# Key side of a two-block attention kernel: every second slot in the order gathering, transposes, keys

## The chip, the cores and the metric

The kernel runs on one core of one Trainium2 chip. The metric is the device time of one execution in microseconds (us), as the median of several runs; lower is better.

## The reference, cut to what matters

The whole program is four residual blocks on `x` (32 batches x 64 x 512): attention, feed-forward, a second attention, and a projection with a small expert mixture. The change touches only work that depends on the context and the weights, and not on `x`: the key side of the second attention block, which this kernel computes first.

```python
def _L1_xattn_ref(q, k, v, Wq, Wk, Wv, Wo, bo, g):     # q from x, k = v = ctx: (32, 64, 512)
    kh = jnp.einsum('bcn,oc->bon', k, Wk).reshape(b, HEADS, DIM_HEAD, -1)
    vh = jnp.einsum('bcn,oc->bon', v, Wv).reshape(b, HEADS, DIM_HEAD, -1)
    kh = jax.nn.softmax(kh, axis=-1)
    context = jnp.einsum('bhdn,bhen->bhde', kh, vh)
    ...
    out = jnp.einsum('bhde,bhdn->bhen', context, qh)
    ...
    out = jnp.einsum('bcn,oc->bon', out, Wo) + bo[None, :, None]
```

The key side yields for each batch a matrix `k.M` that holds `context`, the value weights and `Wo` in one product.

## The kernel before

`program` (L1703) runs the stages one after the other: `key_side` (L214), `attention0`, `feed_forward`, `query_side`, `projection`, `experts`. Each stage is a block in which every engine has a queue of its own, written out by hand; semaphores (`wait_ge`, `then_inc`) are all that orders one engine against another. A stage begins when all engines have left the one before it.

`key_side` works on 16 tiles `t`, each of two batches (128 rows of the context), and each tile in four chunks `c`. The steps of a tile are these, with the line of the instruction:

- `context` (TensorE, L607): four transposes of the context into the bank `psM`; ScalarE copies them to `cT` (`transposed`, L551).
- `keys(t, c)` (TensorE, L617): six matmuls, 64x128 weights against 512 columns, into `psK[c % 2]`, a pair of banks for each of two buffers. Then `keys_max` (VectorE, L411) takes the row maxima, and `exponentials` (ScalarE, L558, two activations with accumulation) writes `ek`. The same buffer of `psK` is written again two chunks later, once the exponentials have read it.
- `turn(t, j, b)` (TensorE, L628): four transposes of `ek` into `psT[b]`, for b = 0 and 1. The copies to `eT` are `turned` on VectorE (L416) for b = 1, and for b = 0 an activation on ScalarE (L586); only at the last chunk, j = 3, is b = 0 VectorE's too.
- `gather(t, j)` (TensorE, L640): two matmuls, 128x64 weights against 512 columns, which add chunk j into the bank `psG`. There is one `psG`: after j = 3 ScalarE copies it to `gT` (L592), and `gather(t, 0)` waits for the copy of the tile before (`gT_ok`, L635).
- `matrix(t)` (TensorE, L649): eight small products of `gT` into `psM`, then one VectorE instruction (L426) into `k.M`. It waits for `gT_ok` and, as `psM` is shared with `context`, for `transposed` of tile t + 2 (`cT_ok`, L646).

The main loop goes over laps `t` (0 to 16) and slots `c` (0 to 3). Slot c of lap t holds the keys of the chunk that lies five chunks ahead, `keys(t + 1 + (c + 1) // 4, (c + 1) % 4)`: chunks 1, 2 and 3 of tile t + 1 in slots 0, 1, 2, and chunk 0 of tile t + 2 in slot 3. TensorE's queue in a lap is: slot 0 keys, transposes, `gather(t - 1, 3)`; slot 1 keys, transposes, `gather(t, 0)`, `context(t + 1)`; slot 2 keys, transposes, `gather(t, 1)`, `matrix(t - 1)`; slot 3 keys, transposes, `gather(t, 2)`.

VectorE's queue follows it: in each slot `keys_max` and then `turned`, with single tasks between (`low`, the low halves of the context, L406; weight magnitudes, L433, in the first laps; statistics of `x`, L440, from lap 6 on). ScalarE's queue in a slot is: copy of `psT[0]` (slots 0 to 2), then the exponentials; in slot 0 behind them the copy to `gT`, in slot 1 behind them the copy to `cT`; in laps 0 to 5 weight magnitudes (L567) behind the exponentials of slots 2 and 3 (in lap 5 only slot 2). GpSimd makes the high halves of the context (L364) and from lap 7 on casts the feed-forward weights (L371 to L376), which SyncE's queue then transposes by DMA.

Of the kernel before, what the change touches and what calls it, by code (L numbers as in the profile page):

```python
# [30 lines left out]
NC = L // P  # L31
BATCHES = 32
TILES = BATCHES * D // P
# [18 lines left out]
def chunk(ap, c, n=P):  # L52
    return ap[:, c * n:(c + 1) * n]
# [7 lines left out]
def wait(eng, sem, value):  # L61

    if not isinstance(value, int) or value > 0:
        eng.wait_ge(sem, value)
# [149 lines left out]
def key_side(nc, a, k):  # L214

    with ExitStack() as ctx:
# [41 lines left out]
        def sums_at(t):  # L258
            return range(3 * t, min(3 * t + 3, UNITS))
# [142 lines left out]
        def _(dve):  # L402
            def low(t):
                dve.wait_ge(hi_ok, t + 1)
                wait(dve, k_ps, NC * (t - 1))
                dve.tensor_tensor(cs_lo[t % 2][:, :], cf[t % 2][:, :], cs_hi[t % 2][:, :], ALU.subtract).then_inc(lo_ok, 1)  # L406

            def keys_max(t, c):
                dve.wait_ge(k_ps, NC * t + c + 1)
                wait(dve, ek_ok, 2 * NC * (t - 1) + 2 * c + 2)  # L410
                dve.tensor_reduce(mk[:, c, :], psK[c % 2][:, :, :], X, ALU.max, negate=True).then_inc(mk_ok, 1)  # L411

            def turned(t, j, b):
                dve.wait_ge(t_ps, 2 * NC * t + 2 * j + b + 1)
                wait(dve, g_ps, NC * (t - 1) + j + 1)
                dve.tensor_copy(eT[b][:, j, :], psT[b][:, :]).then_inc(eT_dve, 1)  # L416

            def sums(t):
                dve.wait_ge(ek_ok, 2 * NC * t + 2 * NC)
                wait(dve, M_ok, t - 1)  # L420
                dve.reciprocal(rl[t % 2][:, :, :], le[t % 2][:, :, :]).then_inc(rl_ok, 1)

            def matrix(t):
                dve.wait_ge(rl_ok, t + 1)
                dve.wait_ge(m_ps, t + 1)
                dve.tensor_tensor(k.M[:, 2 * t:2 * t + 2, :, :], psM[:, :].rearrange("p (c b d) -> p b c d", b=2, d=D),  # L426
                                  rl[t % 2][:, :, :].unsqueeze(3).broadcast_to([P, 2, NC, D]), ALU.mult).then_inc(M_ok, 1)

            def magnitudes(u):
                dve.wait_ge(k.unit_in[u % RING], loads_of(u))  # L430
                n, blocks, src = unit_of(a, u)
                room = unit_room(k, u)
                dve.tensor_reduce(k.wabs[0:room.shape[0], n, u % PAIRS:u % PAIRS + 1], room, X, ALU.add,  # L433
                                  apply_absolute_value=True).then_inc(wa_dve, 1)
# [16 lines left out]
            def biases(n):  # L451

                if n == 0:
                    dve.wait_ge(k.b_in, 16 * 2)
                    dve.tensor_copy(part[:, :, :], brow[:, :, :]).then_inc(row_ok, 1)
                    dve.wait_ge(row_ok, 1)
                    dve.tensor_tensor(rest[:, :, :], brow[:, :, :], part[:, :, :], ALU.subtract).then_inc(row_ok, 1)
                    spread(0, part)
                elif n == 1:
                    dve.wait_ge(row_ok, 4)  # L460
                    dve.tensor_copy(part[:, :, :], rest[:, :, :]).then_inc(row_ok, 1)
                    dve.wait_ge(row_ok, 5)
                    dve.tensor_tensor(rest[:, :, :], rest[:, :, :], part[:, :, :], ALU.subtract).then_inc(row_ok, 1)
                    spread(32, part)
                else:
                    dve.wait_ge(row_ok, 6)
                    spread(64, rest)

            def scales():
                dve.wait_ge(sum_ps, 1)  # L470
                dve.tensor_scalar(k.wmean[:, :], psM[:, 0:3], 1.0 / (FF * L), None, ALU.mult).then_inc(inv_ok, 1)
                dve.wait_ge(inv_ok, 1)
                dve.tensor_scalar(den[:, :], k.wmean[:, :], EPS, None, ALU.add).then_inc(inv_ok, 1)
                dve.wait_ge(inv_ok, 2)
                dve.reciprocal(k.winv[:, :], den[:, :]).then_inc(inv_ok, 1)
# [38 lines left out]
            keys_max(1, 0)  # L514
            for t in range(TILES + 1):
                for c in range(NC):
                    if t + 1 + (c + 1) // NC < TILES:
                        keys_max(t + 1 + (c + 1) // NC, (c + 1) % NC)
                    if t < TILES:
                        if c == NC - 1:  # L520
                            turned(t, c, 0)
                        turned(t, c, 1)
                    if c == 0 and t < TILES:
                        sums(t)
                    if c == 0 and 1 <= t < 4:
                        biases(t - 1)
                    if c == 1 and t + 2 < TILES:
                        low(t + 2)
                    if c == 2 and t > 0:
                        matrix(t - 1)  # L530
                    if c == 3:
                        for u in sums_at(t):
                            if u % 3 == 2:
                                magnitudes(u)
                    if c == 0 and t == CAST - 1:
                        dve.wait_ge(wa_act, UNITS - UNITS // 3)
                        dve.wait_ge(wa_dve, UNITS // 3)
                        dve.tensor_reduce(asum[:, :], k.wabs[:, :, :], X, ALU.add).then_inc(sum_ok, 1)
                    if c == 0 and t == CAST:
                        scales()  # L540
                    if c in (0, 3) and STATS <= t < STATS + TILES // 2:
                        stats(2 * (t - STATS) + c // 3)
                    if c == 1 and t == TILES - 1:
                        vec_x(dve)
# [56 lines left out]
        def _(pe):  # L601
            def context(t):

                pe.wait_ge(lo_ok, t + 1)
                wait(pe, M_ok, t - 2)
                for c in range(NC):
                    mm = pe.transpose(chunk(psM, c), chunk(cf[t % 2], c), k.ident[:, :])  # L607
                mm.then_inc(c_ps, 1)

            def keys(t, c):  # L610

                pe.wait_ge(lo_ok, t + 1)
                wait(pe, ek_ok, 2 * NC * t + 2 * c - 2)
                products = ((k.wk_hi, cs_hi[t % 2]), (k.wk_hi, cs_lo[t % 2]), (k.wk_lo, cs_hi[t % 2]))
                for n, (w, x) in enumerate(products):
                    for b in range(2):
                        mm = pe.matmul(psK[c % 2][:, b, :], w[HALF[b], c * P:(c + 1) * P], x[HALF[b], :],  # L617
                                       start=n == 0, stop=n == 2)
                mm.then_inc(k_ps, 1)
# [11 lines left out]
            def gather(t, j):  # L631

                if j == 0:
                    pe.wait_ge(cT_ok, t + 1)
                    wait(pe, gT_ok, t)  # L635
                if j < NC - 1:
                    pe.wait_ge(eT_act, (NC - 1) * t + j + 1)
                pe.wait_ge(eT_dve, 5 * t + j + 1 + j // (NC - 1))
                for b in range(2):
                    mm = pe.matmul(psG[HALF[b], :], cT[t % 2][:, j, b * D:(b + 1) * D], eT[b][:, j, :], start=j == 0,  # L640
                                   stop=j == NC - 1)
                mm.then_inc(g_ps, 1)
# [56 lines left out]
            pe.wait_ge(w_ok, VO_OK)  # L699
            for t in range(TILES + 1):  # L700
                for c in range(NC):
                    if t + 1 + (c + 1) // NC < TILES:
                        keys(t + 1 + (c + 1) // NC, (c + 1) % NC)
                    if t < TILES:
                        turn(t, c, 0)
                        turn(t, c, 1)
                    if c > 0 and t < TILES:
                        gather(t, c - 1)
                    if c == 0 and t > 0:
                        gather(t - 1, NC - 1)  # L710
                    if c == 1 and t + 1 < TILES:
                        if t == CAST:
                            pe.wait_ge(inv_ok, 1)
                        context(t + 1)
                    if c == 2 and t > 0:
                        matrix(t - 1)
                    if c == 3 and t == CAST - 1:
                        pe.wait_ge(sum_ok, 1)
                        pe.wait_ge(M_ok, t)
                        pe.matmul(psM[:, 0:3], k.ones32[:, :], asum[:, :], start=True, stop=True).then_inc(sum_ps, 1)  # L720
# [1073 lines left out]
```

## Time and profile before

| | us |
|---|---|
| median of 3 runs | 799.75 (798.72 to 800.43) |
| the profiled execution, its device time | 799.84 |
| its span in the trace | 797.8 |
| main loop of the key side, within the span | 22.2 to 223 |

Engines are PE (TensorE matmuls), PEld (its weight loads), DVE (VectorE), ACT (ScalarE), POOL (GpSimd). A view of the stretches of time gives for each engine its busy time and the number of its instructions, then TensorE's granted clock as a share of full speed. In a timeline a row is: start in us, time in us, engine, line, operation, tile written and tiles read, shape, number of instructions merged; a bracket behind it is idle time of that engine before it and what ended that. A row of x8 lasts from the first start to the last end. Ends overlap the next start, since matmuls are pipelined: what a step costs is read from start to start.

### The profile page before, as it was taken

What the parts mean: (1) busy time and instruction counts of PE and PEld (TensorE: products, weight loads), DVE (VectorE), ACT (ScalarE), POOL (GpSimd) and SP (SyncE); (2) the same over time, 40 slices, a digit from 0 to 9 for tenths busy, and PEclk for the clock granted to TensorE, in tenths of its full rate; (3) what the DMA queues carried; (4) which work ended last, traced back from release to release, by engine and by line L of the source; (5) the groups of instructions that cost most, each with busy time, mean ns of one, the idle gap of its engine ahead of it and who ended that gap; (6) DMA issues with size and microseconds to landing.
All of it is one profiled execution on the core that took longest, in us unless ns stands there. A gap on an engine that the chain in (4) does not pass through costs nothing. (4 is left out here: it accounts for less than half of the span.)

```text
span 797.8 us, 17690 instructions
## 1 busy us (share of the span) xinstructions
PE 691.3 (87%) x6633; PEld 358.0 (45%) x6633; DVE 622.4 (78%) x1031; ACT 482.2 (60%) x870; POOL 364.8 (46%) x271
## 2 busy tenths in 40 slices
PE   4999999999967875699999489999999999389944
PEld 2454455545545654244444144444444444145541
DVE  6888788888636676699998398999999999355456
ACT  3878876676436665476776167878788787422100
POOL 2000039999725563022112257767686767333100
PEclk9999999999999998799999779999999999779955
DMA  6235455656253320134332100000000000045305
GB/s 161 77 132 171 154 177 151 152 135 173 55 146 72 83 68 6 21 75 75 75 67 57 31 0 2 1 2 1 2 1 1 2 1 1 1 80 80 53 1 210
DMA packets 94183, 54.90 MB, mean 69 GB/s; under 512 B 78548, under 2 KB 78548, under 8 KB 94100
## 3 DMA queue, kind: packets, MB, share of 16 engines
q1 hardware_dynamic: 93348, 53.25, 26.7%
q8 instruction: 54, 0.88, 0.5%
q10 hardware_dynamic: 752, 0.52, 0.3%
q14 instruction: 29, 0.24, 0.1%
HBM read 32.20 MB, written 4.19 MB: 46 GB/s over the span
## 5 line engine op out<-in xcount | busy, mean ns | idle before, releaser
L1312 POOL TENSOR_TENSOR query_qn<-query_eq,query_rq 128x1024 f32<-128x1024 f32 x64 | 121.8, 1904 | 56.7 <-DVE query_rq L1246 54.9
L558 ACT ACTIVATE keys_ek<-keys_psK,keys_mk 128x512 f32<-128x512 f32 x128 | 86.9, 684 | 38.9 <-DVE keys_mk L411 37.0
L411 DVE TENSOR_REDUCE keys_mk<-keys_psK 128x2 f32<-128x1024 f32 x64 | 77.9, 1217 | 16.7 <-PE keys_psK L617 16.6
L1237 DVE TENSOR_REDUCE query_mq<-query_psQ 128x16 bf16<-128x1024 f32 x64 | 75.6, 1181 | 5.2 <-PE query_psQ L1380 5.0
L1243 DVE TENSOR_REDUCE query_lq<-query_eq 128x16 f32<-128x1024 f32 x64 | 77.2, 1207 | 2.6 <-ACT query_eq L1321 2.5
L1321 ACT ACTIVATE query_eq<-query_psQ 128x1024 f32<-128x1024 f32 x64 | 65.2, 1019 | 22.5 <-PE query_psQ L1393 22.5
L628 PE MATMUL keys_psT<-all_ident,keys_ek 128*128 128x128 f32 x512 | 70.8, 282 | 0.0
L1402 PE MATMUL query_psX<-all_ident,query_qn 128*128 128x128 f32 x512 | 70.7, 282 | 0.0
L1040 POOL TENSOR_SCALAR ff_hr<-ff_h,ff_qs 128x1376 f32<-128x1376 f32 x16 | 22.7, 1416 | 104.4 <-DVE ff_qs L1087 104.4
L640 PE MATMUL keys_psG<-keys_eT,keys_cT 128*64 128x512 f32 x256 | 69.0, 617 | 1.0 <-issue 0.9
L628 PEld LDWEIGHTS keys_psT<-all_ident,keys_ek 128*128 128x128 f32 x512 | 55.5, 142 | 28.2 <-issue 20.0
L1328 ACT ACTIVATE query_qT<-query_psX 128x1024 f32<-128x1024 f32 x64 | 65.4, 1022 | 1.2 <-PE query_psX L1402 1.2
L1412 PE MATMUL query_psF<-query_qT,all_M 128*64 128x512 f32 x256 | 61.8, 604 | 1.1 <-ACT query_qT L1328 1.1
L1402 PEld LDWEIGHTS query_psX<-all_ident,query_qn 128*128 128x128 f32 x512 | 55.5, 142 | 15.7 <-issue 14.3
L376 POOL TENSOR_SCALAR keys_st<-all_ring 128x1024 bf16<-128x1024 f32 (+2 forms) x16 | 60.7, 3796 | 1.3
L1161 PE MATMUL ff_psG<-all_wgT,ff_xT 128*128 128x512 bf16 (+1 forms) x192 | 46.8, 367 | 10.6 <-DMA ff_xT<-ff_xq 10.6
L416 DVE COPY keys_eT<-keys_psT 128x512 f32<-128x512 f32 x80 | 53.1, 680 | 2.9 <-PE keys_psT L628 2.9
L364 POOL TENSOR_SCALAR keys_cs_hi<-all_cf 128x512 f16<-128x512 f32 x16 | 9.9, 621 | 97.0 <-DMA all_cf<-in_ctx_dram 88.2
L1134 ACT ACTIVATE ff_r<-ff_psG,all_sg 128x512 f32<-128x512 f32 (+1 forms) x48 | 30.9, 643 | 36.3 <-PE ff_psG L1161 34.6
L1535 PE MATMUL proj_psH<-all_ring,proj_x_T 128*128 128x512 f16 x192 | 46.1, 392 | 0.0
L1166 PE MATMUL ff_psU<-all_wuT,ff_xT 128*128 128x512 bf16 (+1 forms) x192 | 46.1, 363 | 0.0
L1175 PE MATMUL ff_psD<-all_wdT,ff_hT 128*128 128x512 bf16 (+1 forms) x176 | 42.1, 389 | 4.1 <-DMA ff_hT<-ff_hq 4.1
(246 smaller groups left out, 1438.6 us busy)
## 6 DMA issues: line engine op xcount, KB each, us to landing
all_ring<-in_L_ffn_w_down_dram SPq DMA_DIRECT2D x8, 688.0 KB, 4.7
all_ring<-in_L_ffn_w_gate_dram SPq DMA_DIRECT2D x10, 512.0 KB, 4.9
all_ring<-in_L_ffn_w_up_dram SPq DMA_DIRECT2D x10, 512.0 KB, 3.9
all_x_res<-in_x_dram SPq DMA_DIRECT2D x4, 1024.0 KB, 6.1
att_ctx_n<-in_ctx_dram SPq DMA_DIRECT2D x16, 256.0 KB, 2.9
out_dram<-all_x_res SPq DMA_DIRECT2D x16, 256.0 KB, 2.2
all_cf<-in_ctx_dram SPq DMA_DIRECT2D x15, 256.0 KB, 2.6
att_w_nat<-in_L_ffn_W_dram SPq DMA_DIRECT2D x4, 256.0 KB, 4.5
```

The costliest lines, as they stand in the source:

```text
L376: pool.tensor_scalar(st[v % 2][:, 0:w], r, -ROUND, 0.0, ALU.add, ALU.add).then_inc(cast_ok, 1)
L411: dve.tensor_reduce(mk[:, c, :], psK[c % 2][:, :, :], X, ALU.max, negate=True).then_inc(mk_ok, 1)
L558: act.activation(ek[t % 2][b][:, c, :], psK[c % 2][:, b, :], ACT.Exp, bias=mk[:, c, b:b + 1], accum_out=le[t % 2][:, b, c:c + 1]).then_inc ...
L628: mm = pe.transpose(chunk(psT[b], c), chunk(ek[t % 2][b][:, c, :], j), k.ident[:, :])
L640: mm = pe.matmul(psG[HALF[b], :], cT[t % 2][:, j, b * D:(b + 1) * D], eT[b][:, j, :], start=j == 0, stop=j == NC - 1)
L1237: dve.tensor_reduce(mq[g % 2][:, :, 0:HEADS], psQ[g % 2][:, :, :].rearrange("p b (h d) -> p b h d", d=D), X, ALU.max, negate=True).then_in ...
L1243: dve.tensor_reduce(lq[:, :], eq[g % 3][:, :, :], X, ALU.add).then_inc(lq_ok, 1)
L1312: pool.tensor_tensor(qn[m % 2][:, :, :], eq[m % 3][:, :, :], rq[m % 2][:, :].unsqueeze(2).broadcast_to([P, 2 * HEADS, D]), ALU.mult).then_ ...
L1321: act.activation(eq[g % 3][:, :, :].rearrange("p h d -> p (h d)"), psQ[g % 2][:, :, :].rearrange("p b n -> p (b n)"), ACT.Exp).then_inc(eq ...
L1328: act.activation(qT[t % 2][:, :, c * P:(c + 1) * P], psX[:, :, :].rearrange("p b (j n) -> p (b j) n", n=P), ACT.Copy).then_inc(qT_ok, 1)
L1402: mm = pe.transpose(psX[:, b, j * P:(j + 1) * P], qn[g % 2][:, b * HEADS + 2 * j:b * HEADS + 2 * j + 2, :].rearrange("p h d -> p (h d)"), ...
L1412: mm = pe.matmul(psF[HALF[b], :], k.M[:, 2 * t + b, j, :], qT[t % 2][:, b * NC + j, :], start=j == 0, stop=j == NC - 1)
```

## The change

The slots with odd c get another order. On TensorE the gathering of the slot comes first, then its transposes, then (in slot 1) `context`, and the keys last. Slots 0 and 2 keep theirs. On VectorE `keys_max` moves behind `turned` in the same slots, 1 and 3. ScalarE's, GpSimd's and SyncE's queues are as before, and no instruction is added or removed.

A lap on TensorE then reads: keys, transposes, `gather(t - 1, 3)` | `gather(t, 0)`, transposes, `context(t + 1)`, keys | keys, transposes, `gather(t, 1)`, `matrix(t - 1)` | `gather(t, 2)`, transposes, keys.

```diff
@@ VectorE, lap t, slot c @@
-                    if t + 1 + (c + 1) // NC < TILES:
+                    if c % 2 == 0 and t + 1 + (c + 1) // NC < TILES:
                         keys_max(t + 1 + (c + 1) // NC, (c + 1) % NC)
                     if t < TILES:
                         if c == NC - 1:
                             turned(t, c, 0)
                         turned(t, c, 1)
+                    if c % 2 == 1 and t + 1 + (c + 1) // NC < TILES:
+                        keys_max(t + 1 + (c + 1) // NC, (c + 1) % NC)
@@ TensorE, lap t, slot c @@
-                    if t + 1 + (c + 1) // NC < TILES:
+                    if c % 2 == 1 and t < TILES:
+                        gather(t, c - 1)
+                    if c % 2 == 0 and t + 1 + (c + 1) // NC < TILES:
                         keys(t + 1 + (c + 1) // NC, (c + 1) % NC)
                     if t < TILES:
                         turn(t, c, 0)
                         turn(t, c, 1)
-                    if c > 0 and t < TILES:
-                        gather(t, c - 1)
-                    if c == 0 and t > 0:
-                        gather(t - 1, NC - 1)
                     if c == 1 and t + 1 < TILES:
                         if t == CAST:
                             pe.wait_ge(inv_ok, 1)
                         context(t + 1)
+                    if c % 2 == 1 and t + 1 + (c + 1) // NC < TILES:
+                        keys(t + 1 + (c + 1) // NC, (c + 1) % NC)
+                    if c == 2 and t < TILES:
+                        gather(t, c - 1)
+                    if c == 0 and t > 0:
+                        gather(t - 1, NC - 1)
                     if c == 2 and t > 0:
                         matrix(t - 1)
```

## Rows read from the trace of the kernel before

**Rows 1.** The page: span, TensorE's busy share, its granted clock in 40 slices
```profile
span 797.8 us, 17690 instructions
...
PE   4999999999967875699999489999999999389944
...
PEclk9999999999999998799999779999999999779955
```

**Rows 2.** Stretches of time: laps in the key side, and attention0 behind it
```profile
60.00:110.00 50.00, 49.25 (x359) 24.98 (x357) 39.87 (x56) 39.43 (x95) 2.48 (x4) 1.00 0.51 167
135.00:185.00 50.00, 50.00 (x368) 25.68 (x368) 42.46 (x65) 33.38 (x84) 48.65 (x31) 1.00 0.58 141
224.00:314.00 90.00, 66.81 (x2686) 49.89 (x2686) 57.95 (x109) 53.94 (x91) 49.06 (x52) 0.96 0.33 83
```

**Rows 3.** Timeline of TensorE: laps 3 and 4, slots 1 to 3 and on
```profile
61.94 1.09 PE L628 MATMUL keys_psT<-all_ident,keys_ek 128*128 128x128 f32 x8
63.22 1.08 PE L640 MATMUL keys_psG<-keys_eT,keys_cT 128*64 128x512 f32 x4 [0.19 <-issue]
64.23 0.66 PE L607 MATMUL keys_psM<-all_ident,all_cf 128*128 128x128 f32 x4
64.82 0.39 PE L617 MATMUL keys_psK<-keys_cs_hi,all_wk_hi 64*128 64x512 f16 x2
65.05 0.38 PE L617 MATMUL keys_psK<-keys_cs_lo,all_wk_hi 64*128 64x512 f16 x2
...
65.57 1.09 PE L628 MATMUL keys_psT<-all_ident,keys_ek 128*128 128x128 f32 x8
66.59 1.08 PE L640 MATMUL keys_psG<-keys_eT,keys_cT 128*64 128x512 f32 x4
67.50 1.04 PE L649 MATMUL keys_psM<-all_wv_wo,keys_gT 128*64 128x128 f32 x16
68.48 0.39 PE L617 MATMUL keys_psK<-keys_cs_hi,all_wk_hi 64*128 64x512 f16 x2
...
81.09 0.39 PE L617 MATMUL keys_psK<-keys_cs_hi,all_wk_hi 64*128 64x512 f16 x2
```

**Rows 4.** Timeline of VectorE, lap 3
```profile
65.68 1.22 DVE L411 TENSOR_REDUCE keys_mk<-keys_psK 128x2 f32<-128x1024 f32 x1 [0.85 <-PE keys_psK L617]
...
69.34 1.23 DVE L411 TENSOR_REDUCE keys_mk<-keys_psK 128x2 f32<-128x1024 f32 x1
70.48 1.28 DVE L416 COPY keys_eT<-keys_psT 128x512 f32<-128x512 f32 x2
```

**Rows 5.** Timeline of ScalarE, laps 3 and 4
```profile
62.53 0.59 ACT L592 ACTIVATE keys_gT<-keys_psG 128x512 f32<-128x512 f32 x1
63.01 0.60 ACT L586 ACTIVATE keys_eT<-keys_psT 128x512 f32<-128x512 f32 x1
...
66.94 0.69 ACT L558 ACTIVATE keys_ek<-keys_psK,keys_mk 128x512 f32<-128x512 f32 x1
...
68.28 1.05 ACT L567 ACTIVATE keys_st<-all_ring 128x1024 bf16<-128x1024 f32 x1
...
71.94 1.05 ACT L567 ACTIVATE keys_st<-all_ring 128x1024 bf16<-128x1024 f32 x1
...
72.99 0.59 ACT L586 ACTIVATE keys_eT<-keys_psT 128x512 f32<-128x512 f32 x1
73.52 0.69 ACT L558 ACTIVATE keys_ek<-keys_psK,keys_mk 128x512 f32<-128x512 f32 x1
```

**Rows 6.** Timeline of TensorE, lap 5, slot 1
```profile
87.41 1.09 PE L628 MATMUL keys_psT<-all_ident,keys_ek 128*128 128x128 f32 x8
89.06 1.08 PE L640 MATMUL keys_psG<-keys_eT,keys_cT 128*64 128x512 f32 x4 [0.56 <-issue]
```

## The prediction

> **What bounds the kernel now.** I read the page first for where TensorE is the bound, then the stretches of time, then the timelines of TensorE, VectorE and ScalarE over one lap. The page shows TensorE at nine tenths or more, at full clock, over most of the key side [rows 1]. By stretches it is stricter: TensorE is busy for 49.25 of 50 us in laps 3 to 6 and 50.00 of 50 later, at a granted clock of 1.00, while VectorE has about 40 and ScalarE 33 to 39 of 50 [rows 2]. So in the key side TensorE's own queue sets the pace, and what it has not got is room for a wait. From the keys of slot 3 in lap 3 (68.48) to those in lap 4 (81.09) a lap takes 12.61 us [rows 3].
>
> The timeline of TensorE gives the step from each group to the next: keys to transposes 0.75, transposes to gathering 1.02, gathering to `matrix` 0.91, `matrix` to keys 0.98, gathering to `context` 1.01, `context` to keys 0.59 [rows 3]. Two things can be read from these steps. First, the gathering costs 0.91 when `matrix` follows, whose weights have the same 128x64 shape, and 1.01 when `context` (128x128) follows: about 0.10 us is lost where the shape changes. Second, four transposes alone (`context`) cost 0.59 and eight cost 1.02, so four cost 0.43 and a lone group of them 0.16 more, at its two borders together. A pair of key matmuls takes 0.23 at the head of a group [rows 3]; three pairs without a border are about 0.66.
>
> The waits of today stand in the same rows. `gather(t, 0)` once started 0.26 us later than its 1.02 (61.94 to 63.22): ScalarE's copy `gT` had begun at 62.53, and the gathering began 0.69 after it [rows 3, 5]. In lap 5 the same step is 1.65, so 0.63 late [rows 6]. The same 0.26 occurs in lap 1. This wait on the one bank `psG` is thus already the latest thing before slot 1's gathering, even with a whole key group and the transposes (0.75 + 1.02) between `gather(t - 1, 3)` and `gather(t, 0)`. The change takes this cover away.
>
> **The change, part by part.**
>
> *Borders on TensorE.* Before, a lap has 13 changes of shape (four keys to transposes, four transposes to gathering, gathering to keys twice, gathering to `context`, `context` to keys, `matrix` to keys). After, it has 8: in slots 0 and 2 keys to transposes and transposes to gathering, in slots 1 and 3 gathering to transposes, then `context` or transposes to keys; the pairs keys-keys, gathering-gathering, transposes-`context`, gathering-`matrix` and `matrix`-gathering have equal shapes. Five borders at 0.10 to 0.16, taken as 0.13, are 0.66 us a lap; 15 laps give -9.9. Keys behind keys, gathering behind gathering and transposes behind gathering are orders that no row shows; from below they save nothing (0), from above 5 x 0.16 = 0.8 a lap. I take 0.66, since the one equal-shape neighbour that the rows have, gathering to `matrix`, has no border in spite of a wait at its head.
>
> The Trainium skill, "TensorEngine Tiling (Array Packing)", section Key Properties, says that changing the tiling mode drains TensorE. The trace agrees as far as the 0.91 against 1.01 goes. By this rule alone the change would be a gain: that is the rival of the other sign, below.
>
> *The wait on `psG`.* `gather(t - 1, 3)` now ends slot 0 and `gather(t, 0)` begins slot 1, with nothing between them. The second may not write `psG` before ScalarE has copied it, and on ScalarE that copy is queued behind the exponentials of `keys(t + 1, 1)`. The keys of slot 3 and slot 0 are now adjacent, so all that work comes in one burst. Counting from the start of slot 3's keys: 0.86 until VectorE begins the maxima (64.82 to 65.68), 1.26 until the exponentials begin (to 66.94), 1.34 for them (to 68.28), 0.53 for slot 0's copy of `psT[0]` (72.99 to 73.52), 1.34 for the exponentials of slot 0, 0.69 for the copy `gT` up to the gathering [rows 3 to 5]. The sum is 6.02; with some hundredths for the hand-overs 6.1. VectorE's way is as long where statistics or other small work lie between its maxima (0.86 + 1.14 + some 0.8 + 1.26 + 1.34 + 0.69 = 6.1, with 1.14 from 69.34 to 70.48) [rows 4]. TensorE needs from the same point 0.66 (keys) + 0.75 (keys) + 1.02 (transposes) + 0.91 (gathering) = 3.34. The wait is 2.75 us in laps 6 to 14. In laps 1 to 5 a weight magnitude stands behind slot 3's exponentials on ScalarE, 1.05 (71.94 to 72.99) [rows 5], and the wait is 3.8. Lap 15 has no keys in slot 0, and about 0.9 remains. Together 5 x 3.8 + 9 x 2.75 + 0.9 = 44.7. Queued behind the waiting gathering are slot 1's transposes, `context` and both key groups, and on these VectorE and ScalarE wait in turn: nothing catches the loss up, as the next burst starts from keys that come behind it.
>
> *The wait of `matrix`.* It needs `cT` of `context(t + 1)`, and ScalarE makes it behind the exponentials of slot 1's keys, which TensorE now does last. From the start of those keys: 0.86 + 1.26 + 1.34 + 0.69 = 4.15 [rows 3 to 5], against 0.66 + 0.75 + 1.02 + 0.91 = 3.34 on TensorE. The wait is 0.8 us, in 14 laps 11.3.
>
> *Ends.* In lap 0 `gather(0, 0)` comes straight behind its transposes and waits for their copy, about 0.9; later `gather(0, 2)`, directly ahead of which no `matrix` lies yet, about 1.4. In lap 15 most groups have no keys beside them and wait for copies of 0.6 to 0.7, about 2.2 in all. Together 4.5, bounds 2 and 7. The old waits, 0.26 + 0.26 + 0.63 = 1.15, are inside the new ones and are taken off.
>
> *What is hidden.* `keys_max` moved behind `turned` costs nothing on its own: it moves with its keys. Both VectorE (40 of 50) and ScalarE have time in a lap of 15.5 us [rows 2]. GpSimd's and SyncE's queues aren't touched; in laps 9 to 12 GpSimd is busy for 48.65 of 50 us [rows 2], which would hold back a faster lap, while a lap of 15.5 gives it room, and its casts end before TensorE does. The buffers `psK` come free in time: a key group waits for exponentials two groups back, and these are over before the wait on `psG` is.
>
> **The sum.** -9.9 + 44.7 + 11.3 + 4.5 - 1.2 = +49.4 us. As a cross-check, a lap follows from its chain: 6.1 (keys of slot 3 to `gather(t, 0)`), then 0.96 + 0.93 + 0.53 for gathering, transposes and `context` with their single borders, 4.15 (keys of slot 1 to `matrix`), then 0.86 + 0.96 + 1.02 to the keys of slot 3: 15.5 us against 12.6. The profiled execution took 799.84, its span 797.8, and the median is 799.75, so the same sum stands on either: 799.8 + 49.4 = 849.2, rounded to 849.5 for the hand-overs left out.
>
> **The rivals.**
>
> *The clock falls too.* TensorE is then idle for 3.6 of 15.5 us (23%), where it had been busy throughout. In attention0, where it is busy for 66.81 of 90 us, the granted clock was 0.96 [rows 2], that is, short times at its lower level of 1.2 GHz. At 0.96 over the 250 us of the new key side 20 us would be spent at half clock; some 40% of a lap's chain is TensorE work, each such us of it doing half: 20 x 0.4 x 0.5 = 4, so about 854; with longer falls, as the page shows elsewhere (0.5 to 0.7 of a slice) [rows 1], 860 or more. The Trainium skill, "TensorE: Matmul & The Clock Gate", section A second HAM failure mode: psum-queue depth-cycling, tells of small idle times between groups of matmuls that make the clock go up and down; no run here shows it in this stage.
>
> *A border belongs to every group, not to a change of shape.* Then the -9.9 is gone on paper, but the lap's chain has only two more borders in it, since most of what is saved lies before a wait: 2 x 0.15 x 15 = 4.5, thus 854.
>
> *The waits are shorter.* If ScalarE and VectorE overlap their instructions more in the burst, 0.4 us off each of the two waits gives -12: about 838. The durations in the rows already are spacings under load, which speaks against it.
>
> *Faster.* Mechanism: the five borders are saved and `gT` is there in time. It decides at `gather(t, 0)`: the way over ScalarE would have to take 3.34 us rather than 6.1. Price then -9.9, at best 790, and GpSimd's 48.65 of 50 would keep it at 790 to 794. The 0.26 and 0.63 us of today, with 1.77 us more cover, speak against it [rows 3, 6]. That the order doesn't change what TensorE does (no change) would need a queue that isn't in order, for which no row speaks.
>
> **How the numbers follow.** Forecast 849.5, chance 0.65 (845 to 855 with the ends of the terms); the clock 0.16; borders everywhere 0.07; shorter waits 0.08; faster 0.03; no change 0.01. The range, 840 to 861, takes in the first three and half of the fourth. A measurement of this kernel can tell about 0.2% (1.6 us) from no change; slower than that 0.96, within it 0.01, faster 0.03.
>
> **What would show it.** In the timeline of TensorE: keys-keys at about 0.66 start to start, gathering-gathering separated by an idle time of 2.75 us (3.8 in laps 1 to 5) that ends with ScalarE's L592; `matrix` with 0.8 before it, ended by L551; laps of 15.5 us; the key side's end at about 272 instead of 223; everything behind it as long as before. I would be wrong in mechanism if idle time were spread evenly, if L592 came right behind the gathering without exponentials before it, or if stages behind the key side had changed; in size, if the granted clock of the key side were below 1.00.

## The result, and the profile after

The changed kernel takes 875.85 us (874.27 to 878.81, 4 runs) against 799.24 for the kernel before: a ratio of 1.0958, with a 95% interval of 1.0936 to 1.0979. It is slower, as forecast, but by 76.6 us and not by 49.7; the time lies outside the stated range.

The profiled execution has a span of 874.2 us. The first matmul of attention0, the stage behind the key side, starts at 299.25 us in the changed kernel:

```profile
299.25 0.87 PE L917 MATMUL att_psQK<-all_bias_rows,all_ones 128*128 128x512 bf16 x2 [1.14 <-PEq L216]
```

In the kernel before it starts at 223.24:

```profile
223.24 0.59 PE L911 MATMUL att_psQK<-all_bias_rows,all_ones 128*128 128x512 bf16 x2 [1.14 <-PEq L216]
```

So the key side grew by 76.0 us. What follows it takes 574.9 us, as before (574.6). The whole difference lies in the stage that was changed.

The page of the changed kernel, the rows that answer to [rows 1]: TensorE's busy share and its granted clock in 40 slices of 21.9 us.

```profile
PE   4788777888788778765999975999999999849944
...
PEclk9888899899889899987999996999999999969965
```

From the second slice to the 13th TensorE is down to seven or eight tenths, and the row of the granted clock has eights among its nines there, where it had nines only. The stretches of time say it with two digits (columns as in [rows 2]: PE, PEld, DVE, ACT, POOL, granted clock, DMA share, GB/s).

```profile
22.20:299.00 276.80, 220.93 (x1433) 116.84 (x1431) 160.34 (x241) 136.92 (x342) 103.85 (x61) 0.89 0.35 99
...
232.00:238.00 6.00, 3.75 (x27) 1.63 (x25) 5.68 (x10) 3.63 (x10) 5.83 (x4) 1.00 0.40 122
238.00:241.40 3.40, 3.06 (x10) 1.48 (x11) 0.00 (x0) 0.24 (x2) 0.00 (x0) 0.50 0.00 0
241.50:249.30 7.80, 7.15 (x60) 4.09 (x58) 5.26 (x7) 4.25 (x11) 3.94 (x4) 1.00 0.67 167
```

Over the key side the granted clock is 0.89. Within one lap it is 1.00, then 0.50 for 3.4 us, then 1.00 again. The lower level of 1.2 GHz begins at 238.0, at the end of the wait before `gather(t, 0)`, which starts at 238.34. In these 3.4 us VectorE does nothing: its next copy waits for TensorE's transposes. The timeline of TensorE for that lap, from the keys of slot 3 to the next ones:

```profile
232.25 0.39 PE L619 MATMUL keys_psK<-keys_cs_hi,all_wk_hi 64*128 64x512 f16 x2
...
232.90 0.38 PE L619 MATMUL keys_psK<-keys_cs_hi,all_wk_hi 64*128 64x512 f16 x2
...
233.65 1.09 PE L630 MATMUL keys_psT<-all_ident,keys_ek 128*128 128x128 f32 x8
234.67 1.08 PE L642 MATMUL keys_psG<-keys_eT,keys_cT 128*64 128x512 f32 x4
238.34 1.97 PE L642 MATMUL keys_psG<-keys_eT,keys_cT 128*64 128x512 f32 x4 [2.59 <-ACT keys_gT L594]
240.24 1.64 PE L630 MATMUL keys_psT<-all_ident,keys_ek 128*128 128x128 f32 x8
241.72 0.60 PE L609 MATMUL keys_psM<-all_ident,all_cf 128*128 128x128 f32 x4
242.25 0.39 PE L619 MATMUL keys_psK<-keys_cs_hi,all_wk_hi 64*128 64x512 f16 x2
...
246.41 1.09 PE L651 MATMUL keys_psM<-all_wv_wo,keys_gT 128*64 128x128 f32 x16 [0.65 <-issue]
247.30 1.06 PE L642 MATMUL keys_psG<-keys_eT,keys_cT 128*64 128x512 f32 x4
248.29 1.09 PE L630 MATMUL keys_psT<-all_ident,keys_ek 128*128 128x128 f32 x8
249.31 0.39 PE L619 MATMUL keys_psK<-keys_cs_hi,all_wk_hi 64*128 64x512 f16 x2
```

The starts give the four pieces of the lap:

| piece of the lap | forecast, us | measured, us |
|---|---|---|
| keys of slot 3 to `gather(t, 0)` | 6.1 | 238.34 - 232.25 = 6.09 |
| `gather(t, 0)` to keys of slot 1 | 2.42 | 242.25 - 238.34 = 3.91 |
| keys of slot 1 to `matrix` | 4.15 | 246.41 - 242.25 = 4.16 |
| `matrix` to keys of slot 3 | 2.84 | 249.31 - 246.41 = 2.90 |
| the lap | 15.5 | 17.06 |

Three of four are as forecast to 0.06 us. The second is 1.5 us too long, and it is the one that runs at half clock: the gathering takes 1.90 to the next start instead of 1.0, the eight transposes 1.48 instead of 0.93. The timeline of ScalarE in the same wait shows the queue that the gathering waited for: exponentials, copy, exponentials, and only then the copy `gT`.

```profile
234.37 0.69 ACT L560 ACTIVATE keys_ek<-keys_psK,keys_mk 128x512 f32<-128x512 f32 x1 [3.30 <-DVE keys_mk L411]
...
235.71 0.59 ACT L588 ACTIVATE keys_eT<-keys_psT 128x512 f32<-128x512 f32 x1
236.30 0.69 ACT L560 ACTIVATE keys_ek<-keys_psK,keys_mk 128x512 f32<-128x512 f32 x1
...
237.64 0.59 ACT L594 ACTIVATE keys_gT<-keys_psG 128x512 f32<-128x512 f32 x1
```

The waits of TensorE over the whole key side, as total, number and longest:

```profile
PE keys_psG L642 <- ACT keys_gT L594: 41.4, 15, 3.8
PE keys_psM L651 <- issue: 8.5, 13, 0.7
```

The idle time before `gather(t, 0)` is 3.5 to 3.8 us in laps 1 to 5 and 2.2 to 2.6 us in laps 6 to 14. In each of these 14 laps the clock falls at the end of this time or just behind it.

### The profile page after: what moved, and what is told of

The parts are those of the page before. It is cut to its first block and busy times, and to the rows that moved or that the text cites. A ratio compares the mean times of both kernels' runs of the same rounds, so it can differ in the third digit from the quotient of the medians.

```text
span 874.2 us, 17690 instructions
## 1 busy us (share of the span) xinstructions
PE 714.6 (82%) x6633; PEld 374.1 (43%) x6633; DVE 621.7 (71%) x1031; ACT 478.3 (55%) x870; POOL 364.5 (42%) x271
## 5 line engine op out<-in xcount | busy, mean ns | idle before, releaser
L642 PE MATMUL keys_psG<-keys_eT,keys_cT 128*64 128x512 f32 x256 | 81.6, 715 | 44.3 <-ACT keys_gT L594 41.4
L416 DVE COPY keys_eT<-keys_psT 128x512 f32<-128x512 f32 x80 | 53.4, 685 | 87.0 <-PE keys_psT L630 87.0
L630 PEld LDWEIGHTS keys_psT<-all_ident,keys_ek 128*128 128x128 f32 x512 | 64.9, 159 | 52.2 <-issue 39.9
L630 PE MATMUL keys_psT<-all_ident,keys_ek 128*128 128x128 f32 x512 | 81.3, 309 | 0.8 <-DVE keys_eT L416 0.4
L588 ACT ACTIVATE keys_eT<-keys_psT 128x512 f32<-128x512 f32 x48 | 28.7, 597 | 50.6 <-PE keys_psT L630 50.6
```

The source lines that it names most:

```text
L630: mm = pe.transpose(chunk(psT[b], c), chunk(ek[t % 2][b][:, c, :], j), k.ident[:, :])
```

## The experiments

The kernel before was run again beside the experiments. Its median is 799.90 us (7 runs) beside the filler, slot 1, slot 3 and `gT` first, and 800.23 (20 runs) beside the four others.

Theory C: the waits are as forecast, and the missing 26 us are TensorE's clock, which falls because TensorE is idle. Rival D: the missing time comes from longer queues on ScalarE and VectorE. The single lap above doesn't decide between them for the whole stage, since the waits of the early laps are longer.

**Filler in the wait.** The idle time is filled, everything else stays.

```diff
+            def filler(t):
+                wait(pe, M_ok, t - 1)
+                if t == CAST:
+                    pe.wait_ge(inv_ok, 1)
+                for n in range(28 if t < 6 else 20):
+                    pe.transpose(chunk(psM, n % NC), k.ident[:, :], k.ident[:, :])
...
+                    if c == 1 and 1 <= t < TILES - 1:
+                        filler(t)
                     if c % 2 == 1 and t < TILES:
                         gather(t, c - 1)
```

> The changed kernel with filler transposes in TensorE's queue at the head of slot 1, ahead of gather(t, 0), in laps 1 to 14: 28 of them in laps 1 to 5 (28 x 0.109 = 3.1 us), 20 in laps 6 to 14 (2.2 us). They write psM, which nothing reads at that point; their results are not used, and they lie inside the wait on the copy gT (3.5 to 3.8 and 2.6 us). Theory C (TensorE's clock falls to its lower level because of the idle time, and that is what the forecast under-priced, 1.5 us a lap): the granted clock of the key side is 1.00 or near it, the step from gather(t, 0) to keys is 2.4 instead of 3.9 us, the lap 15.6 instead of 17.07, the time 850 to 853. Rival D (the queues of ScalarE and VectorE lengthen the lap, the clock is beside the point): 875 or more. Rival E (only part of the clock comes back, as 0.4 us before the gathering and 0.8 before matrix stay idle): 858 to 868.

Measured: 851.79 us (849.93 to 853.81), 24.1 us faster than the changed kernel, with 320 transposes (5 x 28 + 9 x 20) more in TensorE's queue. The stretches of time of this kernel:

```profile
22.20:273.00 250.80, 230.35 (x1746) 137.48 (x1746) 160.58 (x241) 136.79 (x341) 102.74 (x61) 1.00 0.40 110
```

And its timeline of TensorE around the wait:

```profile
197.23 1.08 PE L642 MATMUL keys_psG<-keys_eT,keys_cT 128*64 128x512 f32 x4
198.24 2.40 PE L651 MATMUL keys_psM<-all_ident 128*128 128x128 f32 x20
200.90 1.08 PE L642 MATMUL keys_psG<-keys_eT,keys_cT 128*64 128x512 f32 x4 [0.26 <-issue]
201.91 1.09 PE L630 MATMUL keys_psT<-all_ident,keys_ek 128*128 128x128 f32 x8
202.84 0.60 PE L609 MATMUL keys_psM<-all_ident,all_cf 128*128 128x128 f32 x4
203.37 0.39 PE L619 MATMUL keys_psK<-keys_cs_hi,all_wk_hi 64*128 64x512 f16 x2
```

The granted clock is 1.00 over the whole key side, and from `gather(t, 0)` to the keys are 2.47 us (200.90 to 203.37). The time that the gathering waits for hasn't changed: it still starts 6.1 us after the keys of slot 3 (194.80 to 200.90). Theory C is shown, and rivals D and E are out: with the clock restored, and nothing else changed but the filler, 24.1 of the 26.4 us above the forecast are gone.

**Half the filler.** `range(14 if t < 6 else 10)` in its place.

> As the kernel with filler transposes in the wait of slot 1, but half as many (14 in laps 1 to 5, 10 later: 1.5 and 1.1 us). TensorE is then idle for some 2.0 to 2.5 us before gather(t, 0) less 0.1, and 0.8 before matrix. If the clock is a matter of how much TensorE is idle in a lap: 2.3 to 3.1 us idle of 15.6, near the kernel with only slot 1 changed (2.6 of 14.95), which kept its clock from lap 6 on; then 850 to 858, the loss in the early laps. If any wait of over 1.5 us brings the clock down: as the changed kernel, 870 to 876.

Measured: 854.09 us (850.52 to 854.92). The granted clock of the key side is 0.99.

```profile
22.20:275.00 252.80, 216.13 (x1594) 122.33 (x1592) 161.39 (x241) 137.40 (x343) 102.75 (x61) 0.99 0.39 109
```

TensorE is busy 216 of 253 us (85%) here, against 221 of 277 (80%) in the changed kernel, in which part of the busy time is itself stretched by the slow clock. So half the filler was enough for nearly all of the gain. That any wait of over 1.5 us brings the clock down is refuted: in laps 1 to 5 the waits before `gather(t, 0)` are still 1.84 to 2.14 us, and the clock falls in one of the five. That fall, in lap 4, makes the step from `gather(t, 0)` to `matrix` 8.26 us instead of 6.63.

**Slot 1 alone.** The new order only in slot 1 (`c == 1` in place of `c % 2 == 1`, `c != 1` in place of `c % 2 == 0`, on both engines; slot 3 as before).

> Only slot 1 in the new order, slot 3 as before. The wait of gather(t, 0) counts from the keys of slot 0: 0.86 + 1.26 + 1.34 + 0.69 = 4.15 us against 0.75 + 1.02 + 0.91 = 2.68, thus 1.5 (up to 1.9 where VectorE or ScalarE are still busy); matrix waits 0.8 as in the changed kernel. At full clock the lap is 14.4 to 14.9 us, the time 828 to 834. Theory C (clock falls with the idle time): idle is 2.3 to 2.7 us of a lap, less than in the changed kernel, so a part of its 1.5 us a lap comes on top: 835 to 855, with a granted clock between 0.9 and 1.0. Rival D (clock not the cause): 840 to 850 with the clock at 1.0 and longer chains.

Measured: 835.57 us (834.41 to 836.10), a ratio of 1.0448 (1.0430 to 1.0466). It is too fast for rival D (840 to 850). The waits of TensorE, total, number and longest:

```profile
PE keys_psG L642 <- ACT keys_gT L594: 24.3, 15, 2.3
PE keys_psM L651 <- issue: 8.5, 13, 0.7
```

The granted clock of its key side is 0.99. The clock falls in one lap, the fifth, behind a wait of 2.33 us, and the step from `gather(t, 0)` to `matrix` is 8.22 us there instead of 6.63. The time lies 1.6 us above the forecast for full clock (828 to 834) and at the lower end of theory C's 835 to 855.

**Slot 3 alone.** The new order only in slot 3.

> Only slot 3 in the new order, slot 1 as before. The keys of slots 3 and 0 are adjacent, but keys and transposes (1.77 us) lie between the two gatherings: the wait of gather(t, 0) is 6.1 - 3.34 - 1.77 = 1.0 us less what psK's buffer adds, 1.0 more in laps 1 to 5 behind the weight magnitudes; matrix does not wait. Lap 13.3 us, 14.2 in laps 1 to 5: 812 to 816 at full clock. Theory C: idle is below 1 us of a lap, so the clock stays at 1.00 at least from lap 6 on. Rival D: as much as it costs in the changed kernel, half of 26 us too much, 825 or more.

Measured: 813.40 us (811.79 to 814.53), a ratio of 1.0171 (1.0150 to 1.0193), within the expected 812 to 816. The granted clock is 0.99.

```profile
PE keys_psG L642 <- issue: 8.1, 14, 0.7
PE keys_psT L630 <- ACT keys_eT L588: 3.8, 5, 1.0
PE keys_psK L619 <- ACT keys_ek L560: 2.8, 13, 0.2
```

Over the 799.90 of the kernel before, the two halves of the change cost 35.7 and 13.5 us, together 49.2, with a single fall of the clock in their laps; the forecast has 49.4. Both together cost 76.6, and 51.9 where filler holds the clock up. The clock is the part that neither half has alone. That the waits of the two halves add up so closely was not to be expected, and the kernel with filler is the firmer evidence.

**The copy `gT` first.** The changed kernel, ScalarE's queue in slot 0 turned round:

```diff
+                    if c == 0 and t > 0:
+                        act.wait_ge(g_ps, NC * t)
+                        wait(act, m_ps, t - 1)
+                        act.activation(gT[:, :], psG[:, :], ACT.Copy).then_inc(gT_ok, 1)
                     if t + 1 + (c + 1) // NC < TILES:
                         exponentials(t + 1 + (c + 1) // NC, (c + 1) % NC)
-                    if c == 0 and t > 0:
-                        act.wait_ge(g_ps, NC * t)
-                        wait(act, m_ps, t - 1)
-                        act.activation(gT[:, :], psG[:, :], ACT.Copy).then_inc(gT_ok, 1)
```

> The changed kernel, with ScalarE's copy gT of slot 0 ahead of that slot's exponentials. The copy then starts when gather(t - 1, 3) is over and its own queue reaches it: 1.34 of the wait go, and the wait on psG is 1.4 us instead of 2.75 (2.4 instead of 3.8 in laps 1 to 5); matrix waits 0.8 still. At full clock the lap is 14.2 us, the time 829 to 832. Theory C: the clock still falls at times, at idle 2.2 us a lap, 832 to 850. Rival D: 26 us more than 830, thus 856. If the order of ScalarE's queue isn't what holds gather(t, 0) up: no difference to the changed kernel, 875.

Measured: 840.13 us (839.00 to 841.97), 35.7 us less than the changed kernel, above the forecast for full clock (829 to 832) and within theory C's 832 to 850. Its waits and two stretches:

```profile
PE keys_psG L642 <- ACT keys_gT L592: 13.1, 7, 2.5
PE keys_psG L642 <- DVE keys_eT L416: 12.6, 11, 1.3
PE keys_psM L651 <- issue: 8.5, 13, 0.7
```

```profile
60.00:110.00 50.00, 41.22 (x274) 22.37 (x269) 30.67 (x41) 31.13 (x75) 1.85 (x3) 0.90 0.36 119
135.00:185.00 50.00, 43.38 (x320) 22.84 (x316) 37.66 (x60) 28.55 (x75) 46.18 (x27) 1.00 0.56 131
```

The wait on `gT` falls from 41.4 us in total to 13.1, and behind it VectorE's copy of `psT[1]` (L416) is the next latest, up to 1.3 us. From 135 to 185 us, where the weight magnitudes are over and the waits are short, the clock is full; from 60 to 110 us, where they are longer, it is 0.90. The gatherings of laps 1 and 2 show the same wait without a fall and with one (the row lasts 1.08 us at full clock and 1.98 at half):

```profile
40.30 1.08 PE L642 MATMUL keys_psG<-keys_eT,keys_cT 128*64 128x512 f32 x4 [2.18 <-ACT keys_gT L592]
...
55.56 1.98 PE L642 MATMUL keys_psG<-keys_eT,keys_cT 128*64 128x512 f32 x4 [2.18 <-ACT keys_gT L592]
```

The clock falls in laps 2 to 5, and each time the step from `gather(t, 0)` to `matrix` is 8.21 to 8.26 us instead of 6.68 in lap 1: about 6.3 us in all. Without them the time would be about 834, an estimate, so these falls are most of what lies above 832.

**Both copies first.** The same, and in slot 1 the copy `cT` ahead of the exponentials as well.

> The changed kernel, with both copies of ScalarE, gT in slot 0 and cT in slot 1, ahead of their slot's exponentials. The wait of gather(t, 0) is 1.4 us as with gT alone moved, the 0.8 before matrix shrinks to about 0.3 in front of gather(t, 2), whose copy of psT is then the latest. Lap 13.6 us at full clock, the time 821 to 825. Theory: idle is 1.7 us of a lap and the clock stays at 1.00 from lap 6 on. If the chains over ScalarE aren't what delays TensorE: 840 as with gT alone.

Measured: 832.29 us (831.07 to 835.08), above the expected 821 to 825, though 7.8 us below the kernel with `gT` alone moved. The waits name what was under-priced:

```profile
PE keys_psG L642 <- DVE keys_eT L416: 17.2, 24, 2.3
PE keys_psG L642 <- ACT keys_gT L592: 13.1, 7, 2.5
```

The wait before `matrix` is gone, but VectorE's copy ahead of a gathering ends waits of 17.2 us in total. The granted clock of the key side is 0.97, and 0.93 from 60 to 110 us. The trace divides the miss. The clock falls in laps 2, 4 and 5, and the step from `gather(t, 0)` to `gather(t, 2)` is 8.60 to 8.66 us there instead of 7.04 in lap 1: 4.8 us. The later laps take 13.84 us where 13.6 was expected: about 1.7 us in seven laps. Once, at 223.60, the wait is 2.33 us, behind a `low` on VectorE that took 2.82 us instead of 0.68: that lap is 2.1 us longer.

**Context first.** The kernel before, with one exchange in TensorE's queue of slot 1:

```diff
+                    if c == 1 and t + 1 < TILES:
+                        if t == CAST:
+                            pe.wait_ge(inv_ok, 1)
+                        context(t + 1)
                     if c > 0 and t < TILES:
                         gather(t, c - 1)
                     if c == 0 and t > 0:
                         gather(t - 1, NC - 1)
-                    if c == 1 and t + 1 < TILES:
-                        if t == CAST:
-                            pe.wait_ge(inv_ok, 1)
-                        context(t + 1)
```

> The kernel before, with one exchange: in slot 1 the four transposes of context(t + 1) come ahead of gather(t, 0), directly behind the slot's eight transposes. One border less (transposes to context has equal shapes; gathering to context and context to keys become gathering to keys), 0.16 us in 15 laps = 2.4 us, and the copy gT has 0.43 us more time, which takes away the three waits of 1.15 us in all. 799.7 - 2.4 - 1.15 = 796.2, bounds 795.5 and 799. If borders of equal shape cost as much as the others: 798.6 (only the waits go).

Measured: 797.18 us (795.93 to 798.68, 9 runs) against 800.23 for the kernel before (20 runs), a ratio of 0.9963 (0.9950 to 0.9976): 3.05 us faster, within the expected bounds. The interval of the ratio is 796.2 to 798.3 us and leaves out the 798.6 of borders that cost the same between equal shapes. Its timeline of TensorE in slot 1:

```profile
161.12 1.09 PE L628 MATMUL keys_psT<-all_ident,keys_ek 128*128 128x128 f32 x8
162.05 0.60 PE L607 MATMUL keys_psM<-all_ident,all_cf 128*128 128x128 f32 x4
162.58 1.08 PE L640 MATMUL keys_psG<-keys_eT,keys_cT 128*64 128x512 f32 x4
163.59 0.39 PE L617 MATMUL keys_psK<-keys_cs_hi,all_wk_hi 64*128 64x512 f16 x2
```

From transposes to keys are 2.47 us, where the kernel before has 1.02 + 1.01 + 0.59 = 2.62 [rows 3]: the border is worth 0.15 us a lap, and no wait is left before the gathering. It is the fastest kernel of this study.

**Late gathering.** The kernel before, with keys last in slot 1 only, the gathering after `context`, and both copies of ScalarE first:

```diff
@@ TensorE, lap t, slot c @@
-                    if t + 1 + (c + 1) // NC < TILES:
+                    if c != 1 and t + 1 + (c + 1) // NC < TILES:
                         keys(t + 1 + (c + 1) // NC, (c + 1) % NC)
                     if t < TILES:
                         turn(t, c, 0)
                         turn(t, c, 1)
+                    if c == 1 and t + 1 < TILES:
+                        if t == CAST:
+                            pe.wait_ge(inv_ok, 1)
+                        context(t + 1)
                     if c > 0 and t < TILES:
                         gather(t, c - 1)
                     if c == 0 and t > 0:
                         gather(t - 1, NC - 1)
-                    if c == 1 and t + 1 < TILES:
-                        if t == CAST:
-                            pe.wait_ge(inv_ok, 1)
-                        context(t + 1)
+                    if c == 1 and t + 1 + (c + 1) // NC < TILES:
+                        keys(t + 1 + (c + 1) // NC, (c + 1) % NC)
```

On VectorE `keys_max` of slot 1 moves behind `turned`; ScalarE's queue is that of both copies first.

> The kernel before, with slot 1 on TensorE as transposes, context, gather(t, 0), keys, keys_max behind turned in that slot, and on ScalarE both copies (gT, cT) ahead of the slot's exponentials; slot 3 as before. Two borders less a lap than before (keys behind keys, context behind transposes), 0.25 us, and nearly no wait: gT starts right behind gather(t - 1, 3) and has 1.35 us of transposes and context as cover, cT is ready when matrix comes. Lap 12.3 to 12.5, the time 795.5 to 798. If moving the keys to the end of a slot costs by itself, whatever stands around it: 810 or more.

Measured: 799.82 us (797.03 to 802.58, 12 runs), a ratio of 0.9997 (0.9980 to 1.0013): no difference from the kernel before, and so 2 us above the expected 795.5 to 798. That moving the keys to the end of a slot costs by itself (810 or more) is out. Most laps take 12.35 us against 12.61, so the two borders are saved there. What ate the gain in the other laps is in the timeline:

```profile
160.87 0.66 PE L630 MATMUL keys_psT<-all_ident,keys_ek 128*128 128x128 f32 x4
161.84 0.63 PE L630 MATMUL keys_psT<-all_ident,keys_ek 128*128 128x128 f32 x4 [0.31 <-DVE keys_eT L416]
162.30 0.60 PE L609 MATMUL keys_psM<-all_ident,all_cf 128*128 128x128 f32 x4
```

With no keys between slot 0's and slot 1's transposes, the second four of slot 1 wait for VectorE's copy out of `psT[1]`, about 0.5 us (160.87 to 161.84, where the step is 0.49). The profile has five such waits. Four of them lie in laps of 12.7 to 13.0 us, the fifth in the last lap with transposes. Two laps of 12.6 and 12.7 us have no wait in the profile that would explain them. "Nearly no wait" was wrong for `psT`; it was right for `psG`.

## Why the prediction was wrong, point by point

**What bounds the kernel** was right: TensorE's queue, with no room for a wait. With the clock held up by filler, the waits that the change laid on it show up in the time nearly as forecast (851.79 us against 849.5).

**The borders** were right in mechanism and somewhat too large in size. In the changed kernel keys follow keys after 0.65 us (232.25 to 232.90, forecast 0.66) and `matrix` is followed by a gathering after 0.89. A gathering to transposes is 0.99 (247.30 to 248.29), near the forecast 0.96. In the kernel with context first, the one border that was taken away paid 0.15 us a lap. In a lap of the filled kernel (194.80 to 210.44) the steps without waits and filler add up to about 12.05 us, against 12.61 before. This is an estimate that takes 0.91 for the two gatherings whose next step is hidden by a wait. It makes 0.56 us a lap and 8.4 us in 15 laps, not 9.9. What is saved ahead of a wait makes that wait longer, so the saving was buried.

**The wait on `psG`** was forecast at 2.75 and 3.8 us and is 2.59 of idle time in the lap above and at most 3.8; together 41.4 us, forecast 44.7, where idle time counts from the modelled end of the last matmul. Counted as the forecast counts, it is 238.34 - 234.67 - 0.91 = 2.76 us in that lap. Its cause, ScalarE's queue, was shown by turning that queue round: of the 35.7 us that came back, about half are shorter waits before gatherings (44.3 to 26.8 us in all) and about half are the clock, which fell in 4 laps instead of 14.

**The wait of `matrix`** was forecast at 0.8 in 14 laps (11.3 us); measured are 0.65 to 0.7 of idle time in 14, and 4.16 us from keys to `matrix` against 4.15. The sign that was named for it, a wait ended by the copy `cT`, stands in the profile once; in 13 laps the view says `issue`. That the copy is the cause is shown by the kernel with both copies first, where the wait is gone.

**The ends** were near the forecast where they can be read: the gatherings of lap 0 wait 0.88 and 1.09 us, forecast 0.9 and 1.4.

**The sum** of +49.4 was right for a full clock to 2.3 us: the kernel with filler has 851.79 against the forecast 849.5. It had no term for the clock.

**The step that failed** is the clock, which the sum left out and the first rival, "the clock falls too", priced. It was named, but as the less likely case, with a chance of 0.16, and priced at 4 us (10 and more with longer falls) where it cost 24. The prediction had named the sign of this miss: a granted clock of the key side below 1.00. Two terms of its product were mis-sized. The first is how much of the stage runs at half clock. It was taken from attention0, where TensorE is busy for a like share and the clock was 0.96 [rows 2], and gave 20 us; the key side had 0.89, that is 2 x 0.11 x 276.8 = 61 us. The second is what a slow microsecond costs. I took TensorE's share of the lap's chain, 0.4, as if the falls were spread evenly, and so 0.2 us for each. But the slow 3.4 us begin where the wait ends, on the gathering and the transposes that everything else waits for: they cost 1.49 us in the lap shown (3.91 - 2.42), 0.44 for each, and 24.1 / 61 = 0.39 over the stage. Both errors point the same way, 3 times and 2 times. The laps add up to the same: from `gather(t, 0)` to `matrix` are 9.45 us in laps 2 and 4, where the clock stays down longer, and 8.06 to 8.30 us in the other twelve of laps 1 to 14, instead of 6.63 with filler. The excess is 23.7 us in all.

The other rivals did not occur: the waits weren't shorter, keys behind keys have no border (0.65 us), the time did not fall, and it did not stay the same.

The range should have reached to 876. A case in which a bound engine is given regular idle time needs its clock priced as a term of the sum, at half speed for whatever follows the wait.

## What to carry to other kernels

Before two accumulations into one bank are put next to each other, follow the copy that must lie between them through the queue of the engine that makes it: here two pairs of exponentials and a copy stood ahead of it, and 1.8 us of keys and transposes between the two gatherings had been the cover. Grouping work of one shape saved about 0.15 us a border on TensorE here, and it is to be had where the regrouped pieces have no buffer in common (transposes and `context`), not where it makes a burst for the engines behind. Where the clock falls, an idle TensorE costs twice: price the wait, then price the work right after it at 1.2 GHz. If the wait can't go, a few matmuls of no use in it can pay: 24 of the 77 us here.

## What the runs showed of the hardware

How often the clock fell behind the wait before `gather(t, 0)`, with the idle time of TensorE in that wait:

| kernel | laps | waits, us | falls |
|---|---|---|---|
| changed | 1 to 14 | 2.17 to 3.81 | 14 of 14 |
| `gT` first | 1 to 5 | 2.17 to 2.47 | 4 of 5 |
| both copies first | 1 to 5 | 2.18 to 2.48 | 3 of 5 |
| slot 1 alone | 1 to 5 | 1.43 to 2.33 | 1 of 5 |
| half the filler | 1 to 5 | 1.84 to 2.14 | 1 of 5 |
| filler | 1 to 14 | up to 0.60 | none |

Except with both copies first, each lap has 0.65 us of idle time before `matrix` as well. A wait of 2.18 us was followed by a fall in one lap of the kernel with `gT` first and not in another, so the length of that wait alone doesn't decide. What does, no run here tells; it stays open. In attention0 of the kernel before, at a like busy share, the clock had been 0.96 [rows 2]. The Trainium skill, "TensorE: Matmul & The Clock Gate", section A second HAM failure mode: psum-queue depth-cycling, describes short idle times between groups of matmuls that make the clock go down and up again; the changed kernel's trace agrees, with 0.50 for 3.4 us in the lap shown and 0.89 over the key side.

The slow stretch made the lap longer, to 17.06 us, by stretching work that stood directly behind the wait. The filler instructions did not slow ScalarE or VectorE: in the filled kernel the gathering still starts 6.1 us after the keys of slot 3, and both engines are busy as long as before over the key side (ScalarE 136.79 us against 136.92, VectorE 160.58 against 160.34).
